# Up-projection of an expert layer: plain fp32 matmuls in place of three products of split operands

## The reference

```python
u_m = u * mask[:, None, :]
y = jnp.fft.irfft(jnp.fft.rfft(u_m, n=n) * k_f, n=n)[..., :Lq] + u_m * D[:, None]
y = y * mask[:, None, :]                                  # x of the layer below
logits = jnp.einsum('bsd,ed->bse', y, route_w)            # 8 experts
route_weight = one_hot(argmax) * max                      # top 1
h = jnp.einsum('bsd,erd->bser', y, A)                     # 8 x 16 = 128 ranks
wh = route_weight[..., None] * h
out = jnp.einsum('bser,eor->bso', wh, Bw)                 # the up-projection, 128 ranks to 1024
return x + out
```

## Time and profile before

| | us |
|---|---|
| median of 3 runs | 622.37 |
| lowest and highest | 622.35, 623.7 |
| the profiled execution, its own time | 623.93 |
| span of the profiled execution, first to last instruction | 622.1 |
| PE busy | 591.5 (95%) |
| PEld busy | 530.9 (85%) |
| DVE busy | 542.5 (87%) |
| ACT busy | 379.3 (61%) |
| POOL busy | 372.9 (60%) |
| DMA, mean over the span | 125 GB/s |

### The profile page before, as it was taken

How to read it: one execution, slowest core, us unless ns; L and a number is a source line. 1 busy time by engine, 2 the same in 40 slices (tenths; PEclk the granted TensorE clock), 3 DMA queues, 4 the chain that set the end, 5 groups by cost and what they waited for, 6 DMA issues and landing times.

```text
span 622.1 us, 13886 instructions
## 1 busy us (share of the span) xinstructions
PE 591.5 (95%) x3681; PEld 530.9 (85%) x3681; DVE 542.5 (87%) x1436; ACT 379.3 (61%) x1164; POOL 372.9 (60%) x474
## 2 busy tenths in 40 slices
PE   3379999999999999999999999999999999999995
PEld 2268998999899889988998998899899989988984
DVE  7778889988988898899889888988998898889874
ACT  3676656766676666567666766665676667666520
POOL 4465566557656755675576567556755765676520
PEclk9989999999999999999999999999999999999998
DMA  6023534453454345435534543454345345434521
GB/s 137 17 56 108 152 110 128 147 150 96 142 149 132 113 139 153 112 126 146 152 96 139 151 133 110 141 152 114 125 146 152 98 136 151 139 105 140 154 78 67
DMA packets 37074, 77.68 MB, mean 125 GB/s; under 512 B 11836, under 2 KB 20350, under 8 KB 36998
## 3 DMA queue, kind: packets, MB, share of 16 engines
q1 hardware_dynamic: 27846, 43.76, 29.5%
q10 hardware_dynamic: 9152, 33.03, 13.0%
HBM read 43.16 MB, written 33.62 MB: 123 GB/s over the span
## 4 chain that ended last, share of the span: by engine, by line
PE 92%; DVE 4%; issue 2%; POOL 1%; ACT 0%; DMA 0%; POOLq 0%
PE psYo L987 19%; PE psZ L1009 19%; PE psO L987 15%; PE psYe L987 12%; PE psS L987 11%; PE psO L1036 5%; PE psXe L1000 4%; PE psXo L1000 4%; PE psZ L1078 1%; PE psS L1047 1%; DMA logs<-in_L_cond_log_dt_dram 0%; DVE ex L693 0%; POOL Grev L436 0%; POOL wave L426 0%; DVE fraction L803 0%
## 5 line engine op out<-in xcount | busy, mean ns | idle before, releaser
L468 POOL TENSOR_TENSOR Slo<-Sf,Shi 128x384 fp32r<-128x384 f32 x64 | 64.9, 1015 | 210.1 <-ACT Shi L590 210.1
L852 DVE SCALAR_TENSOR_TENSOR brought<-Sf,tab,psS 64x128 f32<-64x128 f32 x256 | 89.0, 348 | 47.3 <-ACT Sf L585 40.9
L1009 PE MATMUL psZ<-Wt,Y 128*128 128x136 f32 x1024 | 129.6, 280 | 0.0
L1009 PEld LDWEIGHTS psZ<-Wt,Y 128*128 128x128 f32 x1024 | 127.8, 191 | 0.1
L531 ACT ACTIVATE Ghi<-Grev 128x256 fp32r<-128x256 f32 x64 | 26.8, 418 | 94.2 <-POOL Grev L436 94.2
L884 DVE TENSOR_TENSOR ost<-psO,xt 128x512 f32<-128x512 f32 x128 | 82.0, 676 | 2.2 <-PE psO L987 2.2
L461 POOL TENSOR_TENSOR Xlo<-xeven,Xhi 128x512 fp32r<-128x512 f32 x64 | 82.8, 1293 | 0.0
L568 ACT ACTIVATE Xhi<-psXe 128x512 fp32r<-128x512 f32 x64 | 38.2, 597 | 38.3 <-PE psXe L1000 38.3
L789 DVE TENSOR_SCALAR whole<-turns_t 128x256 f32<-128x256 f32 x64 | 57.8, 903 | 4.1 <-ACT turns_t L519 4.1
L585 ACT ACTIVATE Sf<-psS 128x128 f32<-128x128 f32 x64 | 17.7, 277 | 66.4 <-PE psS L987 66.4
L987 PE MATMUL psYo<-Xhi,Thi 128*128 128x512 f32 x128 | 55.6, 434 | 0.0
(11 more groups left out here) (194 smaller groups left out, 1670.8 us busy)
## 6 DMA issues: line engine op xcount, KB each, us to landing
xt<-in_x_dram SPq DMA_DIRECT2D x64, 512.0 KB, 4.1
out_dram<-ost ACTq DMA_DIRECT2D x63, 512.0 KB, 4.8
Traw<-kdram SPq DMA_DIRECT2D x64, 128.0 KB, 2.9
kdram<-krow SPq DMA_DIRECT2D x64, 1.0 KB
A_nat<-in_L_ffn_A_dram SPq DMA_DIRECT2D x1, 512.0 KB, 4.9
B_nat<-in_L_ffn_Bw_dram SPq DMA_DIRECT2D x8, 64.0 KB, 3.6
out_dram<-ost SPq DMA_DIRECT2D x2, 256.0 KB, 2.0
lens_i<-in_itok_B_dram SPq DMA_DIRECT2D x1, 64.0 KB, 3.6
```

The lines of the kernel that those rows point to most:

```text
L468: pool.tensor_tensor(Slo[h.s2][:, :], Sf[h.s2][:, :], Shi[h.s2][:, :].bitcast(F32), ALU.subtract).then_inc(slo_done, 1)
L852: dve.scalar_tensor_tensor(brought[to, :], Sf[h.s2][fr, old], tab2[fr, BR, h.n:h.n + 1], psS[to, new], ALU.mult, ALU.add).then_inc(brought ...
L1009: last = pe.matmul(psZ[:, 0:NW], Y[:, j, c, :], Wt[:, 2 * c + j, :], start=(j == 0 and c == 0), stop=(j == 1 and c == NE - 1), skip_group_ ...
```

## The change

`Bw_hi` and `Bw_lo` become one tile `Bt` of plain fp32, copied by ScalarE as `Bw_hi` was; `whi` and `wlo` become one tile `wht` (two buffers) of plain fp32, copied by ScalarE as `whi` was. VectorE's two subtractions (`w_lo` in each step, `Bw_lo` before the steps) go. `up` issues one plain fp32 matmul of 512 columns for each half in place of three float32r products. The waits for `wlo_done` and `blo_set` become waits for `wht_done` and `bt_set`.

```diff
-        Bw_hi = sb("Bw_hi", [P, L], F32R)
-        Bw_lo = sb("Bw_lo", [P, L], F32R)
+        Bt = sb("Bt", [P, L])
...
-        whi = [sb(f"whi{s}", [P, P], F32R) for s in range(2)]
-        wlo = [sb(f"wlo{s}", [P, P], F32R) for s in range(2)]
+        wht = [sb(f"wht{s}", [P, P]) for s in range(2)]
...
-                act.activation(whi[h.s2][:, :], psWh, ACT.Copy).then_inc(whi_done, 1)
+                act.activation(wht[h.s2][:, :], psWh, ACT.Copy).then_inc(wht_done, 1)
...
-            def w_lo(h):
-                need(dve, whi_done, h.n + 1)
-                need(dve, up_mm, (h.n - 1) * 2)
-                dve.tensor_tensor(wlo[h.s2][:, :], psWh, whi[h.s2][:, :].bitcast(F32),
-                                  ALU.subtract).then_inc(wlo_done, 1)
...
-                if head(-1).there:
-                    w_lo(head(-1))
...
-            for j in range(2):
-                dve.wait_ge(bhi_set, j + 1)
-                TT(Bw_lo[:, j * 512:(j + 1) * 512], psY[j][:, :],
-                   Bw_hi[:, j * 512:(j + 1) * 512].bitcast(F32), ALU.subtract).then_inc(blo_set, 1)
...
-                    three(psO[j][:, :], [((whi[h.s2][:, :], wlo[h.s2][:, :]),
-                                          (Bw_hi[:, half], Bw_lo[:, half]))],
-                          True, True).then_inc(up_mm, 1)
+                    pe.matmul(psO[j][:, :], wht[h.s2][:, :], Bt[:, half], start=True, stop=True,
+                              skip_group_check=True).then_inc(up_mm, 1)
```

More of the change, by code:

```diff
@@ L198, in conv_ffn_kernel @@
         b_turned = sem("b_turned")
-        bhi_set = sem("bhi_set")
-        blo_set = sem("blo_set")
+        bt_set = sem("bt_set")
         x_in = [sem(f"x_in{s}") for s in range(4)]
@@ L244, in conv_ffn_kernel @@
         wh_turned = sem("wh_turned")
-        whi_done = sem("whi_done")
-        wlo_done = sem("wlo_done")
+        wht_done = sem("wht_done")
         up_mm = sem("up_mm")
@@ L662, in _ @@
                 act.wait_ge(b_turned, j + 1)
-                act.activation(Bw_hi[:, j * 512:(j + 1) * 512], psY[j][:, :],
-                               ACT.Copy).then_inc(bhi_set, 1)
+                act.activation(Bt[:, j * 512:(j + 1) * 512], psY[j][:, :],
+                               ACT.Copy).then_inc(bt_set, 1)
             t_hi(first[0])
@@ L1006, in project @@
                 if j == 0:
-                    need(pe, wlo_done, h.n)
+                    need(pe, wht_done, h.n)
                 for c in range(NE):
@@ L1055, in within @@
                 if is_head(h, 0):
-                    pe.wait_ge(blo_set, j + 1)
+                    pe.wait_ge(bt_set, j + 1)
                 need(pe, y_masked, h.n * 2 - 1 + j)
@@ L1076, in turn_wh @@
                 need(pe, wh_done, h.n + 1)
-                need(pe, wlo_done, h.n)
+                need(pe, wht_done, h.n)
                 pe.transpose(psWh, wh[:, :], ident[:, :]).then_inc(wh_turned, 1)
             def up(h, ahead):
-                need(pe, whi_done, h.n + 1)
-                need(pe, wlo_done, h.n + 1)
+                need(pe, wht_done, h.n + 1)
                 if ahead.there:
```

## The result

The changed kernel takes 642.65 us (median of 4 runs) against 623.04 us for the kernel before, run beside it: a ratio of 1.0308, with a 95% interval from 1.0282 to 1.0335. One of the four executions, of 652.28 us at a lower granted clock (0.952 against 0.995 or more), is left out of the ratio, and the median of the other three is 642.25 us. The change makes the kernel slower, by 19 to 20 us. The profiled execution took 642.25 us with a span of 640.4.

The account below looks back on a forecast made before the run. TensorE's list, without idle time from 47 to 600 us, bounds the kernel. +0.31 us for each of 63 heads (+19.5 us) and +0.5 us at the end give +20.0 us on 622.37: 642.4 us, range 639.8 to 646 us.

Parts of the forecast that it names:

- The new matmul: Up-projection on TensorE: four plain fp32 records of 512 columns at 429 ns, 1.716 us for each head.
- the control at the lower level: Before the clock rose: float32r takes 0.83 ns a column, one cycle of 1.2 GHz; fp32 transposes 1.64 ns, two cycles.
- The first rival: Long fp32 streams in the up-projection pay float32r's surcharge: 1.872 us, +0.47 us a head, 652.6 us; chance 0.07.
- The rival of a single cycle a column in a long record: Long fp32 records in the up-projection cost one cycle a column: four take 0.94 us, 592.2 us in all; chance 0.03.
- that of one record for each matmul: Each up-projection matmul leaves one record, not two: 0.86 us, -0.54 us a head, about 587 us; chance 0.02.
- the reading of the Trainium skill's page: Two cycles a column for a whole fp32 matmul: up-projection 0.85 us, kernel some 34 us faster.
- The old products: Six float32r products of 512 columns leave TensorE's up-projection: 1.40 us, 0.234 us each, for each of 63 heads.
- Part 3: VectorE loses subtraction `wlo`, 0.28 us a step; costed at nothing in 63 steps, since TensorE has no idle time.
- part 4: VectorE's adds wait for up-projection halves 0.16 and 0.31 us later; the 0.7 us cover before `carry` is twice what is needed.
- The start: Before the steps, two `Bw_lo` subtractions go; `carry` may begin up to 0.3 us earlier, taken as 0.
- The end: Last step, in series: -0.37 us without `wlo`, +0.83 us for fp32 records; net +0.5 us, between -1.2 and +0.6.
- the assumed lower level: Last head's up-projection at 1.2 GHz: four fp32 records take 3.36 to 3.41 us against 2.56 us, +0.83 us.

Follow-up runs that it names:

- an edit that did cost 58 us: The changed kernel with VectorE's `whole` moved from behind `b_lo` to behind `carry` in all steps but the first: 700.55 us, ratio 1.1234.

## Why the prediction was right

**What bounds the kernel.** Right. TensorE stayed without idle time (571.00 of 571 us). A full busy time alone would not have settled it, since it hid 0.17 us a step in the run with `rank` in PSUM; the chain does, with 0.11 us for the transpose of `wh` in both kernels, and so do the runs: time added (0.31 us a step), cut (two products less, 8.53 us a step) or replaced (bf16) on TensorE came out in the total at its start-to-start price.

**The new matmul.** The forecast of 429 ns a record, 1.716 us for each head, is the measured 0.429 and 1.72. The step that carried it was to read two whole cycles a column out of the rows of plain fp32, with the control at the lower level (1.64 ns, two cycles of 1.2 GHz) beside them. The slope between the two short lengths alone, 0.70 to 0.75 ns a column, would not have done it: 115.6 + 376 x 0.75 = 398 ns a record, 1.59 us an up-projection and 12 us in all, outside the range. From 256 to 512 columns the slope was measured as 0.83 ns (216 and 429 ns). The first rival (float32r's 1.10 cycles a column in fp32 too, 0.47 us apart) fell by the spacing, and the bf16 run shows that the surcharge is float32r's own. The rival of a single cycle a column in a long record (592 us) and that of one record for each matmul (587 us) fell by the same rows: 0.43 us, 256 records. So did the reading of the Trainium skill's page "Perfetto Trace Analysis", section "Engine Utilization", by which the kernel would have become 34 us faster: the trace has two cycles a column in each of the two records.

**The old products.** Priced at 1.40 to 1.41 us for six; the growth of 0.31 us was measured as 0.305.

**VectorE at nothing.** Right in the total (643.19 with the subtraction, 642.65 without), incomplete in the reason. Part 3 saw that VectorE was not the bound. It didn't see that `whole` waits for GpSimd and takes up the time set free (1.49 against 1.48 us to its end). VectorE's busy time even rose, from 542.5 to 546.4 us, above all because the two `add`s no longer overlap, now that the second waits for its product (82.0 us for both before, 88.0 after). `wlo` was also needed from 304.15 on, at the start of `up`, and not from 304.6; it was ready 0.9 us ahead all the same.

**Who waits longer.** The second `add` waits for 0.17 us a step (forecast: 0.1 or more) and `carry` for 0.67 us (forecast: 0.7). The cover held. But part 4 looked only at the waits that the up-projection itself feeds. The thinnest cover of the step, `gate`'s lead of 0.25 us over Slo, was not among them; the change did not touch it, and an edit that did cost 58 us. That was not foreseen, and it is the place where a change on VectorE could have come out much worse than forecast.

**The start and the end.** The start was put at 0 and came out at +0.23 us, with the clock's later rise. The end was put at +0.5 us, from -1.2 to +0.6, and came out at -0.84 - 0.32 = -1.16 us beside the 63rd up-projection's own growth. The term that failed is the assumed lower level: the last up-projection ran at 2.4 GHz in 2.00 us instead of 3.4. The -0.37 us for the subtraction in series held (0.42 us from the end of `whi` to TensorE before, 0.04 after). The end (1.66 us below the forecast), the start (0.23 above) and 0.305 in place of 0.31 us a head (0.3 below) make the span 640.4 us where the sum had 642.1. That the forecast of 642.4 lies 0.25 us from the median of 642.65 is therefore partly luck: it added 20.0 us to 622.37, and measured were 19.2 to 19.6 us on top of 623.04.

## What to carry to other kernels

Where one engine's list has no idle time, a change is worth the start-to-start time of its records, and the price of a length that the kernel doesn't have can be carried over from short lengths of the same type and clock, if the slope is first read as a whole number of cycles: the difference between 128 and 136 columns was 10% too low, two cycles a column came out within 1%. A column cost 4.0 cycles in a plain fp32 matmul, 3.3 in three float32r products and 3.1 in three bf16 products; at full TensorE the split is the cheaper one although it needs more instructions and more preparation. Before anything is moved on VectorE, list for each all-SBUF operation how far it lies ahead of GpSimd's next start; a lead of 0.25 us here was worth 58 us. And a busy time of 100% on TensorE doesn't exclude a short wait in every step: compare the step's chain, piece by piece.

## What the runs showed of the hardware

- float32r streams 512 columns in 0.234 us at 2.4 GHz (1.10 cycles a column) and bf16 in 0.22 us; at 1.2 GHz float32r takes one cycle (0.32 us for 384 columns).
- Plain fp32 takes two cycles a column in each of its two records: 116 ns at 136 columns, 216 at 256 (1.73 us for eight), 429 at 512, and 0.42 us for 256 columns at 1.2 GHz (3.37 us for eight).
- VectorE's `gate` on 8 columns takes 0.29 us alone and up to 1.13 us when it comes up with GpSimd's subtraction, with all operands in SBUF; with its input in PSUM it takes 0.28 us in the same place, in all of 47 and 54 steps.
- TensorE was counted busy for 499.64 of 500 us while its chain lost 0.17 us in every step to a late weight load.
- After the same idle gaps (1.37 and 0.37 us), the last matmuls of a kernel ran at the upper level in one execution and at the lower one in another, worth 1.4 us here (2.00 against 3.37).
